# Counting edges by groups of six nodes and two rows, with one comparison of two tensors for four one-hots

## The reference

```
for i in range(3):
    src_feat = h[edge_src]
    max_val = segment_max(src_feat, edge_dst)
    agg = max_val + log(segment_sum(exp(src_feat - max_val[edge_dst]), edge_dst))
    h_new = concatenate([h, agg]) @ W_l[i].T + b_l[i]
    h = 0.5 * h + 0.5 * relu(layer_norm(h_new))
```

## Time and profile before

| what | value |
|---|---|
| median of 3 runs | 3612.53 us (3607.04 to 3618.94) |
| the profiled execution | 3614.43 us, its span 3612.2 us |
| PE, DVE, ACT, POOL busy over the span | 82%, 45%, 38%, 44% |
| PE busy in 300 to 700 us | 92 to 93% |
| DVE busy in 300 to 700 us | 100% |
| ACT busy in 300 to 700 us | 82% |
| clock granted to TensorE there | 1.00 |

### The profile page before, as it was taken

How to read it: one execution, slowest core, us unless ns; L and a number is a source line. 1 busy time by engine, 2 the same in 40 slices (tenths; PEclk the granted TensorE clock), 3 DMA queues, 4 the chain that set the end, 5 groups by cost and what they waited for, 6 DMA issues and landing times.

```text
span 3612.2 us, 59613 instructions
## 1 busy us (share of the span) xinstructions
PE 2970.1 (82%) x17152; PEld 2102.1 (58%) x17152; DVE 1628.9 (45%) x3492; ACT 1389.0 (38%) x2083; POOL 1591.1 (44%) x1667
## 2 busy tenths in 40 slices
PE   3799999985986985788888898888888888888855
PEld 2577777765986985444554555445455454555455
DVE  7999999985015017322222222222222222222227
ACT  2788888872001001233333333333333333333312
POOL 4000000000000000777777777777777777777642
PEclk7899999997996995788878778888878888787756
DMA  3122222234973961466666666666666666666510
GB/s 115 72 124 107 124 107 124 107 148 190 395 320 139 395 264 57 118 165 164 163 163 166 164 161 167 168 164 162 166 163 166 164 166 164 164 164 165 140 35 18
DMA packets 352485, 576.87 MB, mean 160 GB/s; under 512 B 41884, under 2 KB 248862, under 8 KB 333384
## 3 DMA queue, kind: packets, MB, share of 16 engines
q1 hardware_dynamic: 299480, 467.64, 38.6%
q0 software_dynamic: 52976, 108.89, 14.0%
HBM read 388.48 MB, written 187.88 MB: 160 GB/s over the span
## 4 chain that ended last, share of the span: by engine, by line
POOL 31%; PE 24%; issue 18%; DVE 17%; DMA 7%; DVEq 2%; ACT 1%; POOLq 1%; ACTq 0%; SPq 0%
POOL arena L541 29%; PE ps L665 11%; DVE arena L1330 9%; DMA arena<-p_tab,m_idx 6%; PE ps L742 4%; PE ps L584 3%; PE ps L751 2%; PE ps L739 2%; PE ps L572 1%; DVEq L1330 1%; POOL ends L509 1%; PE ps L759 1%; DVE arena L1317 1%; DVE ybuf L1202 1%; DVE ends L1023 1%
## 5 line engine op out<-in xcount | busy, mean ns | idle before, releaser
L541 POOL DMA_INDIRECT arena<-p_tab,m_idx x1568 | 1486.5, 948 | 1864.6 <-issue 1832.3
L1406 DVE TENSOR_TENSOR_SCAN arena<-arena,ps 128x512 f32<-128x512 f32 x392 | 501.6, 1280 | 1036.5 <-ACT ps L922 937.8
L742 PEld LDWEIGHTS ps<-ident,arena 128*128 128x128 f32 x3136 | 488.0, 237 | 623.2 <-DMA arena<-p_tab,m_idx 463.9
L742 PE MATMUL ps<-ident,arena 128*128 128x128 f32 x3136 | 579.6, 342 | 278.6 <-DMA arena<-p_tab,m_idx 278.6
L917 ACT ACTIVATE arena<-ps 128x512 f32<-128x512 f32 x392 | 234.0, 597 | 1030.1 <-PE ps L742 1017.2
L665 PE MATMUL ps<-arena 128*128 128x192 bf16 (+1 forms) x5635 | 505.6, 248 | 66.7 <-DVE arena L1275 65.8
L751 PE MATMUL ps<-arena,weights 128*128 128x512 f32 x784 | 540.5, 782 | 0.0
L665 PEld LDWEIGHTS ps<-arena 128*128 128x128 f16 x5635 | 481.8, 98 | 81.1 <-issue 66.1
L1330 DVE TENSOR_SCALAR arena<-iota_w,arena 128x392 bf16<-128x392 f16 x2156 | 519.5, 314 | 0.0
L682 PE MATMUL ps<-arena 128*128 128x392 bf16 x2352 | 452.1, 336 | 70.9 <-DVE arena L1330 70.6
L739 PE MATMUL ps<-arena,weights 17*128 17x512 f32 x784 | 487.7, 704 | 0.0
(11 more groups left out here) (187 smaller groups left out, 1675.8 us busy)
## 6 DMA issues: line engine op xcount, KB each, us to landing
arena<-count_d SPq DMA_DIRECT2D x66, 1568.0 KB, 8.2
arena<-keep_d SPq DMA_DIRECT2D x392, 256.0 KB, 4.5
scan_rows<-arena SPq DMA_DIRECT2D x392, 256.0 KB
count_d<-arena SPq DMA_DIRECT2D x49, 1568.0 KB, 5.2
wide<-count_d SPq DMA_DIRECT2D x32, 1568.0 KB, 8.4
arena<-p_tab,m_idx POOLq DMA_INDIRECT x1568
arena<-attr_in SPq DMA_DIRECT2D x392, 34.0 KB
p_tab<-wide SPq DMA_DIRECT2D x7, 448.0 KB, 3.0
```

The lines of the kernel that those rows point to most:

```text
L541: pool.indirect_dma_start(m_rows[:, k, t, :], None, p_tab, bass.IndirectOffsetOnAxis(ap=m_idx[:, k, t:t + 1].bitcast(U32), axis=0))\
L742: last = pe.matmul(x[:, t * P:(t + 1) * P], m_rows[:, k, t, :], ident[:, :], start=False, stop=(t == TB - 1), skip_group_check=True)
L1406: dve.tensor_tensor_scan(m_scan[:, k % SCAN_RING, :], m_mask[:, k, :], m_term[k % TERM_RING], before, ALU.mult, ALU.add).then_inc(e1.scan_ ...
```

## The change

- A window is now 6 nodes (`WD`), a block has `WB` = 22 of them (the last two have 4 nodes), and a window takes `WT` = 2 rows of edges. `WCOLS` is 294. A block has 44 counting matmuls of 294 columns where it had 48 of 392.
- The four destination one-hots of a pair of windows are made by one comparison of two tensors with 294 x 4 elements. The four are interleaved, so the matmul reads its moving operand with a step of 4 elements. `hot_a` and the keys are fp16 now, with room for two pairs; ACT makes no one-hot.
- A source comparison serves 11 windows (22 rows, 2816 elements), two per block, ahead of the comparisons of pairs 3 and 9.
- PE does the sums of the block before in 19 parts of two or three matmuls, one behind each window from the fourth to the last.
- In the setup there are 10 columns of 110 lanes: DVE searches 5 and ACT 5, POOL fetches 10 rows and then 20 rows of edges, the keys are made in 10 groups, and nine small steps on DVE compute each window's first node. `iota_w` and `iota_s` hold each number 4 and 22 times. The semaphores `alone` become one.

```diff
-WD = 8
-WB = P // WD
-WT = 3
-GE = 32
+WD = 6
+WB = -(-P // WD)
+LAST_WD = (P - (WB - 2) * WD) // 2
+BLOCKS = 5
+WQ = BLOCKS * WB
+WG = -(-J // BLOCKS)
+WT = 2
+GE = 8
+PAIRS = WB // 2
+PAIR_COLS = 2 * WT
+BATCH = WB // 2
+HOT_COLS = BATCH * WT
+SUMS_FROM = 3
...
+                def count_window(j, k, r):
+                    w = WB * j + k
+                    slot, b = (WB * r + k) % WSLOTS, k // BATCH
+                    if k % BATCH == 0:
+                        pe.wait_ge(src_hot_ready, 2 * j + b + 1)
+                    if k % 2 == 0:
+                        pe.wait_ge(bank_free, w // 2 + 1 if isinstance(w, int) else PAIRS * j + k // 2 + 1)
+                    if k % 2 == 0:
+                        pe.wait_ge(hot_ready, PAIRS * j + k // 2 + 1)
+                    for i in range(WT):
+                        last = pe.matmul(ps[:, 4 + slot, 0:WCOLS], hot_b[b][:, :, (k % BATCH) * WT + i], hot_a[:, slot // 2, :, (k % 2) * WT + i],
+                                         start=(i == 0), stop=(i == WT - 1))
+                    last.then_inc(win_counted, 1)
...
-                        for q in range(QUADS):
-                            count_windows(j + 1, q)
-                            if q == 0:
-                                first_sums_ready(j)
-                            if q < QUADS - 1:
-                                block_sums(j, r, first_parts, q * J // (QUADS - 1), (q + 1) * J // (QUADS - 1))
+                        for k in range(WB):
+                            count_window(j + 1, k, 1 - r)
+                            if k == SUMS_FROM:
+                                first_sums_ready(j)
+                            if k >= SUMS_FROM:
+                                n = k - SUMS_FROM
+                                block_sums(j, r, first_parts, n * J // (WB - SUMS_FROM), (n + 1) * J // (WB - SUMS_FROM))
...
-                        if m % 2 == 1 and not (last and m == WB // 2 - 1):
-                            one_hot(QUADS * j + m // 2 + 1)
...
-                            for t in range(min(WT, DVE_HOTS - WT * s)):
-                                dve.tensor_scalar(hot_a[:, s, t, :], iota_w[:, :], keyT_a[:, t, bass.ds(w, 1)], None, ALU.is_equal)\
-                                    .then_inc(hot_ready, 1)
+                def one_hots(j, r):
+                    for k in range(WB):
+                        w, slot = WB * j + k, (WB * r + k) % WSLOTS
+                        if k % 2 == 0:
+                            dve.wait_ge(win_counted, w + 2)
+                        if k == BATCH // 2 + 1:
+                            source_hots(j, 1)
+                        if k == BATCH + BATCH // 2 + 1:
+                            source_hots(j + 1, 0)
+                        if k % 2 == 0:
+                            keys = keyT_a[:, bass.ds(w, 2), :].rearrange("p w i -> p (w i)")
+                            dve.tensor_tensor(hot_a[:, slot // 2, :, :], iota_w[:, :, :], keys.unsqueeze(1).to_broadcast([P, WCOLS, PAIR_COLS]),
+                                              ALU.is_equal).then_inc(hot_ready, 1)
```

More of the change, by code:

```diff
@@ L131, in build @@
         node_no, after_node, sign_sum = (sb(n, [P, J]) for n in ("node_no", "after_node", "sign_sum"))
-        iota_w, iota_s = sb("iota_w", [P, WCOLS], FP16), sb("iota_s", [P, P, QUAD], BF16)
+        iota_w = sb("iota_w", [P, WCOLS, PAIR_COLS], FP16)
         extreme = sb("extreme", [P, 2 * D])
@@ L191, in build @@
                   .bitcast(FP16).rearrange("p (a d) -> p a d", a=J) for r in range(RING)]
[L192 to L199, removed]
+        keyT_a = carve(at, WT * NW // 2).bitcast(FP16).rearrange("p (w i) -> p w i", i=WT)
+        keyT_b = carve(at + WT * NW, WT * NW // 2).bitcast(BF16).rearrange("p (w i) -> p w i", i=WT)
+        hot_at = at + WT * NW + WT * NW // 2
+        hot_a = carve(hot_at, WSLOTS * WT * WCOLS // 2).bitcast(FP16)\
+            .rearrange("p (s c n) -> p s c n", s=WSLOTS // 2, n=PAIR_COLS)
+        hot_b_at = hot_at + WSLOTS * WT * WCOLS // 2
+        hot_b = [carve(hot_b_at + n * (HOT_COLS * P // 2), HOT_COLS * P // 2).bitcast(BF16).rearrange("p (c n) -> p c n", n=HOT_COLS)
+                 for n in range(2)]
+        over_stage = stage[:, :, :, :].rearrange("p s t f -> p (s t f)")
+        iota_s = over_stage[:, 2 * GT * P - HOT_COLS * P // 2:2 * GT * P].bitcast(BF16).rearrange("p (c n) -> p c n", n=HOT_COLS)
         first_parts = carve(2 * BLK // 2, J * FIRST_COLS // 2 + 1).bitcast(BF16)[:, 0:J * FIRST_COLS]\
@@ L317, in build @@
         gate_in, gate_done, x_summed = (sem(n) for n in ("gate_in", "gate_done", "x_summed"))
-        alone = {e: sem("alone_" + e) for e in ("sp", "act", "pe", "pool", "dve")}
+        alone = sem("alone")
         block = ctx.enter_context(nc.Block())
@@ L569, in turn @@
                 pe.wait_ge(node_copied, n + 1)
-                pe.sem_inc(alone["pe"], 1)
+                pe.sem_inc(alone, 1)
                 for t in range(GT):
@@ L1098, in _ @@
             dve.sem_inc(h_ready, 1)
+            link(dve.tensor_copy(iota_s[:, :, :], iota_i[:, 0:P].unsqueeze(2).to_broadcast([P, P, HOT_COLS])))
             dve.wait_ge(edges_loaded, 2 * DMA)
@@ L1105, in _ @@
             dve.tensor_scalar(keep_l, keep_l, -1.0, 1.0, ALU.mult, ALU.add).then_inc(masks_ready, 1)
-            link(dve.tensor_scalar(win_base[:, :], win_base[:, :], float(WCOLS), None, ALU.mult))
-            link(dve.tensor_copy(iota_w[:, :], iota_i[:, :]))
-            link(dve.tensor_copy(iota_s[:, :, :], iota_i[:, 0:P].unsqueeze(2).to_broadcast([P, P, QUAD])))
+            link(dve.tensor_scalar(win_base[:, :], win_base[:, :], float(J), -1.0, ALU.mult, ALU.add))
+            link(dve.tensor_scalar(iota_i[:, :], iota_i[:, :], 1.0, None, ALU.add))
+            link(dve.tensor_copy(iota_w[:, :, :], iota_i[:, :].unsqueeze(2).to_broadcast([P, WCOLS, PAIR_COLS])))
             link(dve.scalar_tensor_tensor(bound[:, :], V("gamma"), -1.0, V("gamma"), ALU.mult, ALU.max))
-            babs = stage[:, 0, 0:LAYERS, 0:D]
+            babs = ybuf[:, 0:LAYERS, :]
             beta = V("beta").rearrange("p (l d) -> p l d", l=LAYERS)
@@ L1471 @@
     src[:N_EDGES] = a["src"]
-    dst = np.full(EPAD, NPAD, i32)
+    dst = np.full(EPAD, NO_DST, i32)
     dst[:N_EDGES] = a["dst"]
```

136 lines of the change are left out of this document (58 added, 78 removed).

## The result

| | us |
|---|---|
| before, median of 4 runs | 3613.56 (3607.04 to 3618.94) |
| after, median of 4 runs | 3870.05 (3867.32 to 3874.21) |
| ratio, with 95% interval | 1.0712 (1.0691 to 1.0732) |
| predicted | 3638 (3590 to 3690) |

The change makes the kernel 7% slower. The direction was forecast; the size, 257 us instead of 25, was not. The profiled execution of after has a span of 3868.2 us. By stage it stands against that of before, which was 3612.2 us long, like this. The first source comparison starts at 131.3 us instead of 108.9 (+22.4). From there to the last read of the sums (1058.6 us, before 799.2) the counting takes 927.3 us instead of 690.3 (+237.0). All that follows takes 2809.6 us instead of 2813.0 (-3.4).

What follows compares the result with a forecast made beforehand. DVE's own work was taken to bound the counting stage. The profiled 3614.4 us + 18.2 (48 blocks) - 2.1 (first block) + 9.7 (setup) gave 3640.2; that execution lay 1.9 over the median, so 3638 us, range 3590 to 3690.

Steps and rivals of the forecast that it cites:

- Count matmuls: Counting stage on PE: 0.128 us per matmul of 294 columns, interpolated between rows for 392 and 195 columns.
- rival (c): Counting matmuls: a moving operand with a step runs slower, +2.9 to 3.4 us a block, 3777 to 3801 us; chance 0.07.
- The block's steps: Counting stage: PE and DVE traced through one block, with three PE waits of about 1.3 us, giving 14.32 us against 13.94.
- hand-overs: Between PE and DVE in each block: 0.33 us from PE to DVE, 0.10 us from DVE to PE.
- DVE's work: Counting stage: pair comparison 0.77 us, source comparison 1.61 us, DVE's own work 10.8 us a block.
- rival (d): DVE's pair comparison runs at one element a cycle, 0.61 us more each, at least 3792 us; chance 0.02.
- Setup, +9.7: Setup before counting: extra search, fetches, casts and key groups cost +9.7 us, bounds +5 and +13.
- (a): Counting stage: PE's waits on source comparisons are not there, block 11.7 us, 3513 us; chance 0.13.
- (b): Counting stage: hand-overs or comparisons a little shorter, block 13.7 to 14.0 us, 3608 to 3623 us; chance 0.14.
- Rival (e): Counting stage: clock drops to half in one stretch per two blocks, +24 us, 3662 us; chance in full 0.04.
- The first block: First block of the counting stage, which has no sums: 11.6 us against 13.7, so -2.1 us.
- 0.38 forecast: Counting stage: each block 14.32 us instead of 13.94, 0.38 us more, +18.2 us over 48 blocks.

Runs made afterwards that it cites:

- the two edits that take waits away: On the kernel with a 4-byte step, sums ended four windows before the last (ratio 0.9988), then a third pair-comparison buffer added (ratio 0.9823).
- the kernel with three buffers: Changed kernel with 4-byte step, sums ending behind window 17 and a third pair-comparison buffer: ratio to the kernel before 0.9823, on another chip 0.9852.

## Why the prediction was wrong

- **Count matmuls, "a straight line between the two gives 0.128 us for 294 columns": this term failed.** The line was drawn through operands without a step, and the new one has a step of 8 bytes; measured 0.262 us, and 0.125 for the same 294 columns without the step. The trace had the warning beside it, the stationary operand that loads in 143 instead of 98 ns with a step. The prediction put the case as rival (c), gave it 0.07 and let a rule stand against the row: the Trainium skill (SBUF — State Buffer, the note on cachelines) has 16-bit data read for free up to a step of 8 elements. The runs contradict it for TensorE's moving operand at 3, 4 and 7 elements (0.20, 0.262 and 0.445 us); only 2 are nearly free (0.133). Where a page of the Trainium skill and the nearest row point in different directions, the row deserved more than 7%.
- **Rival (c)'s price** was too small: +2.9 to 3.4 us a block, measured +4.07. It had put 28 of the 44 matmuls on the path, at 0.10 to 0.12 us. In fact the extra is 0.137 us and PE becomes the bound: 44 x 0.262 + 4.3 = 15.8 us of its own work, and two of its three waits stay. Its work and its waits (2.3 us a block) are 18.1 of the 18.88 us; the rest is not accounted for.
- **The block's steps** were right. Without a step a block is 14.81 us (forecast 14.32), with each wait at its place. Of the missing 0.49 us, 0.18 is the jump back of the loop, which I hadn't counted, and 0.3 dearer hand-overs. That DVE's saving goes into waits is shown by the two edits that take waits away: 15.10 to 13.44 to 12.18 us.
- **DVE's work**: 0.768 and 1.62 us for the comparisons against 0.77 and 1.61. Right; rival (d) is out.
- **Setup, +9.7** (its parts add up to 9.8): right, +8.3 to +8.7 by like pace. The rest of the 22.4 us is the slow input product of that execution. The forecast had no term for it.
- **Rivals (a)**, no waits, and **(b)**, a block of up to 14.0 us: out by rows.
- **Rival (e)**, a falling clock: it came, and cost the changed kernel next to nothing. The clock is 0.92 over its counting stage, and 40 of the 47 blocks between two reads of the sums have a stretch at half clock, but those are no longer than the others. The counts don't feel it, and the wait in front of pair 3 takes the rest back: with such a stretch in front of it (the block from 488.67 on) pair 3 starts 4.92 us after pair 0, without one (from 507.37 on) 4.91. Two blocks of after:

```profile
751.66:770.73 19.07, 16.55 (x93) 10.59 (x93) 11.65 (x15) 7.11 (x12) 0.00 (x0) 0.91 0.20 84
789.44:808.51 19.07, 16.34 (x93) 10.42 (x93) 11.65 (x15) 7.11 (x12) 0.00 (x0) 1.00 0.20 84
```

  With a step of 4 bytes, where a count does feel it, such a block is 0.25 to 0.6 us longer (two of that kernel: 15.17 us without such a stretch, 15.41 with one). Without a step the clock over the stage is 0.99 to 1.00.
- **The first block**, -2.1 us: wrong for the changed kernel. From the first source comparison to the first read of the sums, which is this block and one more, it is 28.8 us before, 34.7 after and 28.6 in the kernel without a step. Less one block each that leaves 14.8, 15.9 and 13.8 us: the step took back what the block had won, and without it the gain is 1.1 us, half of the forecast.
- **The sum** with what was measured: 48 x (0.38 forecast + 0.49 hand-overs and loop + 4.07 for the step of 8 bytes) = 237 us, and 22.4 of setup, less 3.4: 256, the difference of the two spans. The three block terms add up to the measured 18.88 - 13.94 us by the way they were taken, so this sum checks the arithmetic only.

**Open**: what is behind the counting stage, the same instructions in all, took between 2801 and 2843 us in the profiled executions on the chips that run the kernel before in 3607 to 3614 us. So the kernel with three buffers is 92 us ahead at the last read of the sums (721.0 against 813.4 us, profiled on the same chip) and 66 at the end of the span (3547.8 against 3614.3). 87 of the 92 us are the counting stage itself (603.7 against 690.4 us); the rest is that this execution of the kernel before had the slow input product and the other had not. What lies behind took 2826.8 us against 2800.9, and no run here explains that. The second chip's 4174 us, too, were not looked into.

## What to carry to other kernels

Price a change of layout at the reader as well as at the writer: interleaving made VectorE's comparison cheap and doubled the cost of each matmul that reads it. Interleave 16-bit moving operands by two at most (0.133 against 0.125 us a count here), and let the same instruction write the rest of its output apart. Where two engines alternate over a short ring of buffers, add up the hand-overs before the work, and keep what one engine reads from the other's last instruction a few steps behind it.

## What the runs showed of the hardware

- A moving operand of 16 bits with a step costs as if about 9 bytes of memory were walked over per ns and partition, whatever of it is used: 0.133, 0.20, 0.262 and 0.445 us for 294 columns at 4, 6, 8 and 14 bytes, the last at a granted clock of 0.50.
- This price doesn't change with the clock, while the pace of the columns does: 0.262 us at 8 bytes at a granted 1.00 and at 0.54, and 0.20 against 0.246 us at 6 bytes at 1.00 and at 0.50.
- fp16 moving against bf16 stationary costs nothing (0.262 us with either type, 0.125 without a step).
- A comparison of two 16-bit tensors keeps its pace with 4 and with 2 keys in a run (768 and 767 ns for 1176 elements, 949 for 1536 with 12 in a run).
- The jump back of a loop body showed as 0.37 us per pass on the path, where DVE and PE wait for each other; before, with DVE always busy, blocks were 13.94 us apart without exception.
